# Reordering the first ramp of a three-layer transformer kernel: four buffers for rounded weights, parts of gate/up behind their own weight groups

## The reference, cut to what matters

```python
def fp4_quant_dequant(x):                       # blocks of 16 along the last dimension
    scale = max(max(abs(block)) / 6, 1e-12)
    q = GRID[searchsorted(MID, abs(block / scale))] * sign(block) * scale
    # GRID 0 .5 1 1.5 2 3 4 6
def fp4_linear(x, w):
    return einsum('bsk,nk->bsn', fp4_quant_dequant(x), fp4_quant_dequant(w))
def ffn(x):
    h = silu(fp4_linear(x, w_gate)) * fp4_linear(x, w_up)     # 256 -> 704
    return fp4_linear(h, w_down)                              # 704 -> 256
x = x + 0.5 * ffn(layernorm(x))
x = x + attention(layernorm(x))                 # complex projections Wq, Wk, Wv, Wo with biases
x = x + 0.5 * ffn(layernorm(x))
```

## Time and profile before

| | |
|---|---|
| Median of 3 runs | 894.83 us (894.54 to 894.95) |
| The profiled execution | 895.14 us, span 893.3 us |
| TensorE busy | 872.8 us, 98% of the span |
| VectorE busy | 708.2 us, 79% |
| ScalarE busy | 626.4 us, 70% |
| POOL busy | 570.5 us, 64% |
| Chain that ended last | TensorE 93% of the span |

### The profile page before, as it was taken

One profiled execution on the slowest core, in us unless ns is written; L12 is line 12 of the kernel. 1 busy time (PEld: TensorE's weight loads), 2 busy tenths in 40 slices (PEclk: granted clock), 3 DMA queues, 4 the chain that ended last, 5 costly groups with the idle time before them and its releaser, 6 DMA issues.

```text
span 893.3 us, 14660 instructions
## 1 busy us (share of the span) xinstructions
PE 872.8 (98%) x4836; PEld 753.7 (84%) x4836; DVE 708.2 (79%) x1104; ACT 626.4 (70%) x1394; POOL 570.5 (64%) x640
## 2 busy tenths in 40 slices
PE   4999999999999999999999999999999999999997
PEld 3788999999988788888888788888888999999996
DVE  6987999999977897855656646455688999999997
ACT  5889888987685866758686786758775676555543
POOL 5477889988640554536658454636676878877762
PEclk9999999999999999999999999999999999999999
DMA  9200000000000000000000000000000000000001
GB/s 313 73 1 1 1 1 1 2 1 1 1 1 1 1 1 1 0 1 1 1 1 1 1 1 1 1 1 1 1 1 1 1 25 25 24 25 25 1 24 48
DMA packets 11948, 13.73 MB, mean 15 GB/s; under 512 B 864, under 2 KB 11104, under 8 KB 11872
## 3 DMA queue, kind: packets, MB, share of 16 engines
q1 hardware_dynamic: 11872, 12.79, 4.3%
HBM read 8.59 MB, written 4.19 MB: 14 GB/s over the span
## 4 chain that ended last, share of the span: by engine, by line
PE 93%; DVE 2%; ACT 2%; DMA 1%; issue 1%; POOL 0%; SPq 0%; DVEq 0%; ACTq 0%; POOLq 0%
PE bank L2035 27%; PE bank L2299 20%; PE bank L2362 19%; PE bank_b L2046 7%; PE bank L1912 7%; PE bank_b L2053 5%; PE bank L2289 2%; PE bank L2107 1%; PE bank_b L2107 1%; DMA wk_s<-in_L_attn_Wk 1%; PE bank L1908 1%; PE bank L1919 1%; PE bank_b L1912 0%; ACT s_ring L1738 0%; DVE grid L915 0%
## 5 line engine op out<-in xcount | busy, mean ns | idle before, releaser
L690 POOL TENSOR_TENSOR p_lo<-s_ring,p_hi 128x512 fp32r<-128x512 f32 x128 | 167.1, 1309 | 186.3 <-ACT p_hi L1749 185.8
L638 POOL TENSOR_TENSOR zq<-grid,s_neg 128x256 f32<-128x256 f32 (+2 forms) x184 | 142.2, 802 | 12.8 <-DVE grid L915 12.0
L2035 PE MATMUL bank<-w_hi,T_hi 128*128 128x512 f32 (+1 forms) x384 | 149.7, 390 | 0.2 <-DVE z L874 0.2
L2035 PE MATMUL bank<-w_lo,T_hi 128*128 128x512 f32 (+1 forms) x384 | 144.0, 375 | 0.0
L2035 PE MATMUL bank<-w_hi,T_lo 128*128 128x512 f32 (+1 forms) x384 | 144.0, 375 | 0.0
L2362 PE MATMUL bank<-p_hi,xv 128*128 128x512 f32 x512 | 141.1, 393 | 0.3 <-DVE p_lo L1074 0.3
L1092 DVE TENSOR_TENSOR top<-bank,top 128x512 f32<-128x512 f32 x92 | 63.4, 690 | 93.5 <-ACT s_ring L1732 91.8
L1732 ACT ACTIVATE s_ring<-bank 128x512 f32<-128x512 f32 x128 | 76.0, 594 | 73.4 <-PE bank L2299 66.9
L1537 ACT ACTIVATE T_hi<-bank 128x1024 fp32r<-128x1024 f32 (+1 forms) x68 | 64.7, 952 | 80.6 <-PE bank L1912 80.3
L2362 PEld LDWEIGHTS bank<-p_hi,xv 128*128 128x128 f32 x512 | 94.0, 188 | 18.6 <-issue 0.7
L620 POOL TENSOR_TENSOR y<-z,s_inv 128x960 f32<-128x960 f32 (+1 forms) x56 | 99.8, 1782 | 6.6 <-DVE rounded L909 5.9
(11 more groups left out here) (242 smaller groups left out, 1926.9 us busy)
## 6 DMA issues: line engine op xcount, KB each, us to landing
out<-x SPq DMA_DIRECT2D x7, 512.0 KB, 2.9
x<-in_L_attn_hidden_states SPq DMA_DIRECT2D x3, 1024.0 KB, 12.2
x<-in_L_attn_hidden_states SPq DMA_DIRECT2D x2, 512.0 KB, 7.5
wraw<-in_L_ffn_w_down SPq DMA_DIRECT2D x1, 704.0 KB, 7.5
wraw<-in_L_ffn_w_up SPq DMA_DIRECT2D x1, 640.0 KB, 5.5
wq_s<-in_L_attn_Wq SPq DMA_DIRECT2D x1, 512.0 KB, 7.1
wk_s<-in_L_attn_Wk SPq DMA_DIRECT2D x1, 512.0 KB, 8.0
wo_s<-in_L_attn_Wo SPq DMA_DIRECT2D x1, 512.0 KB, 8.4
```

Of the source, the lines that this page charges most:

```text
L638: last = nc.gpsimd.tensor_tensor(out=blocks(zq[:, to:to + hi - lo]), in0=blocks(grid[:, lo:hi]), in1=spread(s_neg[:, par, lo // BLOCK:hi / ...
L690: nc.gpsimd.tensor_tensor(out=lower_buf(n, c), in0=score_buf(n, c), in1=upper_buf(n, c).bitcast(F32), op=ALU.subtract).then_inc(plo_done, 1)
L2035: last = nc.tensor.matmul(gu[:, lo:hi], lhsT=T[:, par, HK + kd, :], rhs=w[:, kd, lo:hi], start=n == 0, stop=n == len(terms) - 1)
```

## The change

- wy gets four buffers. All six weight_y run on POOL (0 to 3 first, ahead of weight_q(0); 4 and 5 behind first_ffn(-4)), none on VectorE; weight_y(i) waits for the rounding of piece i - 4, and one semaphore counts them.
- The addition of eps leaves POOL for the first two groups: ScalarE does it for tiles 0 to 3, VectorE for tiles 4 to 7, between first_blocks(-3) and weight_grid(5).
- VectorE: weight_scales is split in weight_maxima and weight_inverses; for the down weights the rounding of chain step -3 stands between the two.
- ScalarE: weight_abs(2) between the variances of tiles 1 and 2; all four sums of tiles 4 to 7 ahead of upper_group(0); normalise(0) ahead of upper_group(1); chain_upper(-4) and chain_rest(-4) ahead of upper_group(5) and lower_group(4); lower_group(5) behind m_upper, m_lower behind it and normalise(2) behind that.
- TensorE: transpose_group(0) and (1) ahead of key_query_rest(0); chain_lower(-4) ahead of weight_lower(5); gate_up(0, 0) waits for 4 lowered groups, gate_up(0, 1) for 5, gate_up(0, 2) for all; query_row(2) and (3) behind gate_up(0, 1).

The diff, cut to its core:

```diff
-        wy = sb("wy", [P, 2, I], at=ffn)
+        wy = sb("wy", [P, 4, I], at=ffn)
...
             def group_std(g):
-                if g != 2:
+                if g > 2:
                     pool.wait_ge(x_var, input_variances(4 * g + 3))
                     nc.gpsimd.tensor_tensor(out=var[:, q], in0=var[:, q], in1=eps_all[:, q],
                                             op=ALU.add).then_inc(x_eps, 1)
+                if g != 2:
                     pool.wait_ge(x_eps, g + 1 if g < 2 else g)
...
             def weight_y(i):
                 pool.wait_ge(wc["inv"], SCALED[i])
-                if i >= 2:
-                    pool.wait_ge(wc["abs"], i - 1)
-                    pool.wait_ge(wc["rnd"], i - 1)
+                if i >= 4:
+                    pool.wait_ge(wc["abs"], i - 3)
+                    pool.wait_ge(wc["rnd"], i - 3)
...
-            weight_y(0)
-            weight_y(1)
-            weight_y(2)
+            for i in range(4):
+                weight_y(i)
             weight_q(0)
             weight_q(1)
             group_std(0)
...
             first_ffn(-4, 0)
-            pool.wait_ge(wc["y"], 2)
+            weight_y(4)
             weight_y(5)
             group_std(1)
...
+            def variances_with_eps(g):
+                q = slice(4 * g, 4 * g + 4)
+                dve.wait_ge(x_var, 4 * g + 4)
+                nc.vector.tensor_scalar(out=var[:, q], in0=var[:, q], scalar1=EPS, scalar2=None,
+                                        op0=ALU.add).then_inc(x_eps, 1)
...
             weight_grid(0)
             weight_grid(1)
-            weight_y(3)
             weight_grid(2)
             weight_grid(3)
             first_blocks(-6, 0)
             first_blocks(-5, 1)
             dve.wait_ge(wd_in, 16)
-            weight_scales(4, 4, NW)
-            first_blocks(-4, 0)
-            weight_y(4)
+            weight_maxima(4, NW)
+            first_to_grid(-3)
+            weight_inverses(4, 4, NW)
+            first_scales(-2, 0)
+            first_scaled(-2)
             first_product(0)
             weight_grid(4)
             first_blocks(-3, 1)
+            variances_with_eps(1)
             weight_grid(5)
...
+            def first_variances_with_eps():
+                act.wait_ge(x_var, 4)
+                nc.scalar.activation(var[:, 0:4], var[:, 0:4], ACT.Copy, bias=EPS).then_inc(x_eps, 1)
...
-            x_variances(0, 4)
+            x_variances(0, 2)
             weight_abs(2)
+            x_variances(2, 4)
+            first_variances_with_eps()
             weight_abs(3)
-            x_sums(4, 6)
+            x_sums(4, 8)
             upper_group(0)
+            normalise(0)
             upper_group(1)
-            normalise(0)
             lower_group(0)
             lower_group(1)
-            x_sums(6, 7)
             upper_group(2)
             upper_group(3)
...
+            chain_upper(-4, 0)
             upper_group(5)
-            chain_upper(-4, 0)
+            chain_rest(-4, 0)
             lower_group(4)
-            lower_group(5)
-            chain_rest(-4, 0)
             absolute(-3)
             m_upper()
+            lower_group(5)
+            m_lower()
             normalise(2)
-            x_sums(7, 8)
-            m_lower()
             minus_means(1)
             silu_gate(0)
...
             key_query_product()
-            key_query_rest(0)
             transpose_group(0)
             transpose_group(1)
+            key_query_rest(0)
             key_query_rest(1)
...
             query_row(1)
+            chain_lower(0, -4, 0)
             weight_lower(5)
-            chain_lower(0, -4, 0)
-            query_row(2)
-            query_row(3)
-            pe.wait_ge(wc["lo"], G1)
+            pe.wait_ge(wc["lo"], 4)
             wait_lowered(0, -4)
             gate_up(0, 0)
             key_query_lower()
+            pe.wait_ge(wc["lo"], 5)
             gate_up(0, 1)
+            query_row(2)
+            query_row(3)
             transpose_chain(0, -3)
+            pe.wait_ge(wc["lo"], G1)
             pe.wait_ge(aw["m_lo"], 1)
             gate_up(0, 2)
```

More of the change, by code:

```diff
@@ L197, in macaron_kernel @@
         x_in_s = [sem(f"x_in{n}") for n in range(len(x_parts))]
-        wc = {k: sem("w_" + k) for k in ("amax", "up", "neg", "inv", "y", "y_pool", "abs", "rnd", "grid", "q", "T", "hi",
+        wc = {k: sem("w_" + k) for k in ("amax", "up", "neg", "inv", "y", "abs", "rnd", "grid", "q", "T", "hi",
                                          "sub", "lo")}
@@ L422, in weight_groups @@
                        wd_hl[:, k:k + 2, 0:D], wd_hl[:, k:k + 2, D:], NW)
-        Y_MADE = {0: ("y_pool", 1), 1: ("y_pool", 2), 2: ("y_pool", 3), 3: ("y", 1), 4: ("y", 2), 5: ("y_pool", 4)}
         SCALED = (1, 2, 3, 3, 4, 4)
@@ L557, in weight_y @@
                 pool.wait_ge(wc["inv"], SCALED[i])
-                if i >= 2:
-                    pool.wait_ge(wc["abs"], i - 1)
-                    pool.wait_ge(wc["rnd"], i - 1)
-                nc.gpsimd.tensor_tensor(out=blocks(wy[:, i % 2, :]), in0=blocks(wraw[:, i * I:(i + 1) * I]),
+                if i >= 4:
+                    pool.wait_ge(wc["abs"], i - 3)
+                    pool.wait_ge(wc["rnd"], i - 3)
+                nc.gpsimd.tensor_tensor(out=blocks(wy[:, i % 4, :]), in0=blocks(wraw[:, i * I:(i + 1) * I]),
                                         in1=spread(wsm[:, 3, i * HB:(i + 1) * HB], HB),
-                                        op=ALU.mult).then_inc(wc["y_pool"], 1)
+                                        op=ALU.mult).then_inc(wc["y"], 1)
             def bias_column():
@@ L811, in _, with weight_maxima @@
             dve.wait_ge(sixths, 2)
-            def weight_scales(n, first, last):
+            def weight_maxima(first, last):
                 c = slice(first * HB, last * HB)
@@ L816, in weight_scales, with weight_inverses @@
                                         op=ALU.max, apply_absolute_value=True).then_inc(wc["amax"], 1)
+            def weight_inverses(n, first, last):
+                c = slice(first * HB, last * HB)
                 dve.wait_ge(wc["amax"], n)
@@ L824, in weight_scales @@
                 dve.wait_ge(wc["inv"], n)
-            def weight_y(i):
-                if i >= 2:
-                    dve.wait_ge(wc["abs"], i - 1)
-                    dve.wait_ge(wc["rnd"], i - 1)
-                nc.vector.tensor_tensor(out=blocks(wy[:, i % 2, :]), in0=blocks(wraw[:, i * I:(i + 1) * I]),
-                                        in1=spread(wsm[:, 3, i * HB:(i + 1) * HB], HB),
-                                        op=ALU.mult).then_inc(wc["y"], 1)
+            def variances_with_eps(g):
[3 more added lines that the diff above has]
+                                        op0=ALU.add).then_inc(x_eps, 1)
             def weight_grid(i):
                 wabs_i = wabs[i % 2 if i < 4 else 0]
-                made, count = Y_MADE[i]
-                dve.wait_ge(wc[made], count)
+                dve.wait_ge(wc["y"], i + 1)
                 dve.wait_ge(wc["abs"], i + 1)
@@ L840, in weight_grid @@
                     dve.wait_ge(wc["grid"], i)
-                nc.vector.scalar_tensor_tensor(out=wrnd[:], in0=wabs_i, scalar=ROUND, in1=wy[:, i % 2, :],
+                nc.vector.scalar_tensor_tensor(out=wrnd[:], in0=wabs_i, scalar=ROUND, in1=wy[:, i % 4, :],
                                                op0=ALU.max, op1=ALU.add).then_inc(wc["rnd"], 1)
@@ L1019, in ffn_step @@
                 return step, blocks_of, product, residual_last, scales, to_grid, scaled, lower
-            first_ffn, first_blocks, first_product, first_residual_last, *_ = ffn_step(0)
+            (first_ffn, first_blocks, first_product, first_residual_last, first_scales, first_to_grid, first_scaled,
+             _) = ffn_step(0)
             second_ffn, _, second_product, _, scales, to_grid, scaled, second_lower = ffn_step(1)
             dve.wait_ge(gate_in, 16)
-            weight_scales(1, 0, 1)
+            weight_maxima(0, 1)
+            weight_inverses(1, 0, 1)
             dve.wait_ge(mixed_in, 16 * 3)
-            weight_scales(2, 1, 2)
+            weight_maxima(1, 2)
+            weight_inverses(2, 1, 2)
             dve.wait_ge(up_in, 16)
-            weight_scales(3, 2, 4)
+            weight_maxima(2, 4)
+            weight_inverses(3, 2, 4)
             weight_grid(0)
             weight_grid(1)
-            weight_y(3)
             weight_grid(2)
@@ L1329, in weight_abs @@
             def weight_abs(i):
-                made, count = Y_MADE[i]
-                act.wait_ge(wc[made], count)
+                act.wait_ge(wc["y"], i + 1)
                 if i >= 2:
                     act.wait_ge(wc["grid"], i - 1 if i < 5 else i)
-                nc.scalar.activation(wabs[i % 2 if i < 4 else 0], wy[:, i % 2, :], ACT.Abs,
+                nc.scalar.activation(wabs[i % 2 if i < 4 else 0], wy[:, i % 4, :], ACT.Abs,
                                      scale=ROUND).then_inc(wc["abs"], 1)
```

## The result

The changed kernel takes 895.89 us as a median of 20 runs (895.26 to 897.40), the kernel before 894.81 us in the 20 runs beside them (894.37 to 895.38). The ratio is 1.0014, with an interval of 1.0008 to 1.0021: 1.1 us slower, which is clear of the interval but inside the 0.2% that the text ahead took as no change. The prediction was 895.6 us.

What follows compares the result with a forecast made beforehand. The ramp bounds the kernel: TensorE's matmuls until 31.7 us, then VectorE's list until 49.1 us. Profiled 895.14 + 0.8 (of it 0.2 from product(0)) - 0.31 = 895.6 us as a median; range 894.0 to 897.0 us.

Steps and rivals of the forecast that it cites:

- TensorE's stretch: TensorE's matmuls from 12.8 to 31.7 us, up to product(0): product(0) 0.1 to 0.3 us later, taken as 0.2.
- the list of signs: Times and waits expected in the new trace, such as gate_up(0, 0) at 26.1 and product(0) at 31.8 to 32.0 us.
- the power: POOL's power for tiles 4 to 7, behind VectorE's eps addition: not before 36.5 us, taking 1.20 us (1.04 to 1.20).
- that sign: At VectorE's product(0): a start ahead of 31.4 us would show the prediction wrong.
- TensorE's wait ahead of the transposes: Ahead of the first transposes, TensorE waits for weight_q(1) from 16.38 to about 16.85 us, 0.47 us.
- The term that was off is the first: On TensorE ahead of product(0): gate_up(0, 0) starts at about 26.15 in place of 27.05 us, 0.9 us earlier.
- VectorE's stretch: VectorE's list from 31.7 to 49.1 us: the eps addition delays the maxima, 0.9 us later, 0.2 of it from product(0).
- The 0.31: In the final sum: the median, 894.83 us, lies 0.31 us below the profiled execution, 895.14, so 0.31 is subtracted.
- (1): Ahead of product(0): TensorE's waits do go, product(0) up to 1.3 us earlier, 894.2 us; chance 0.18.
- (2): TensorE's early matmuls: a 0.47 us wait makes the clock rise later, 1.7 us over the forecast, 897.3 us; chance 0.12.
- (3): Ahead of product(0): POOL's weight_y(4) and (5) hold VectorE's scaled(-2), product(0) 0.2 to 0.4 us later still, 896.0 us; chance 0.14.
- (4): Whole ramp: nothing lasts, the eps addition costs only 0.1 us and TensorE's wins and losses cancel, 894.9 us; chance 0.14.

Runs made afterwards that it cites:

- the control: The kernel before, unchanged, profiled a second time; its clock rose 3.9 us after TensorE's first matmul, tile 1's gate/up at 19.33 us after that matmul.
- after: The changed kernel with the whole change, against the kernel before: median 895.89 us, ratio 1.0014.
- The first trace: The kernel before, unchanged, in the profile that the prediction used: 895.14 us, clock rising 6.2 us after TensorE's first matmul.
- e10: The changed kernel with one wait added: POOL starts weight_y(5) only behind VectorE's scaled(-2); 895.30 us (1.0014).
- e2: The changed kernel with key_query_rest(0) put back ahead of transpose_group(0) and (1); 895.82 us (1.0014).
- e9: The changed kernel with POOL adding eps for tiles 4-7, query_row(2), (3) behind value_output_product(1), weight_y(5) behind scaled(-2), weight_q(5) behind tile 1's inverses; 894.32 us (0.9998).
- e11: The changed kernel itself run and traced once more, nothing altered; 895.53 us (1.0014).

## Why the prediction was right

**The frame held.** The end moves as the ramp moves: +0.86 at tile 2, +0.86 at the last matmul. The ramp has TensorE's stretch up to product(0) and VectorE's list behind it. The absolute times in the list of signs did not hold: gate_up(0, 0) came at 25.45 us for 26.1, the power at 35.89 for 36.5 or later, tile 2's gate/up at 42.52 for 43.4. product(0), at 31.22 us, even lies ahead of the 31.4 that was to show the prediction wrong. All these stood on a trace with a late start and a late clock. Counted from the first matmul that sign was at 31.4 - 12.83 = 18.57 us, and product(0) came at 18.67; the control, with the clock of after, has it at 18.29. The waits named among the signs are there: VectorE's idle time ahead of the maxima (0.32 us for about 0.5), and TensorE's wait ahead of the transposes.

**TensorE's stretch.** The forecast was a product(0) 0.1 to 0.3 us later, taken as 0.2; by the control it is 0.37 later, with the sign and the reason right (gate_up(0, 0) starts earlier, the rows cost it again). The term that was off is the first: gate_up(0, 0) came 0.70 us earlier, not 0.9. The first trace, counted in the same way, would say 1.32, but it had the late clock. And the stretch from it to product(0) grew by 0.37 + 0.70 = 1.07 us, 0.96 for the rows and 0.1 for the change of form, of which the forecast had up to 0.2. weight_q(1) ended at 16.35 us for 16.61, by its own path as worked out, since the loads of this execution landed 0.25 us earlier. The wait ahead of the transposes was 16.40 - (12.55 + 3.55) = 0.30 us, not 0.47, as the hand-over from POOL took 0.05 us and not 0.24.

**VectorE's stretch.** The forecast was 0.7 us from the addition (0.9 less product(0)'s 0.2, with bounds of 0.45 and 0.8); it is 0.47. The chain ran as described: VectorE's place, POOL's power, nmr, normalise(4), maxima. The addition started 35.65 - 31.22 = 4.43 us behind product(0), where the text had 36.37 - 31.93 = 4.44. From there to the maxima it put 2.43 us, and 37.85 - 35.65 = 2.20 it was. The mis-sized term is the power, 1.01 us, near the short one of the two durations in the earlier trace rows, for which I had taken the long one, 1.20. The traces show that this is no chance: it took 1.01 us in all seven traces that have the addition on VectorE, where it starts behind VectorE's scaled(-1), and 1.12 to 1.20 us in the seven others, where scaled(-1) comes in the middle of it. By moving the addition the change also moved the power. This error and product(0)'s, of opposite signs, nearly cancel, which is luck: 0.8 us forecast, 0.86 in the traces.

**The number.** 895.14 + 0.8 - 0.31 = 895.6 for a measured 895.89. The 0.31 took the profiled execution for slightly slow; it was (a late clock, 0.6 us), and quick between 480 and 490 us (0.5 us). What the sum lacked is the fall of the clock. The 13 runs of after in which it stays have a median of 895.74, and all 20 have 895.89.

**The rivals.** (1) The waits of TensorE did not go: product(0) is later. (2) The clock did not rise late; the pair of key_query_rest at 19.33 us runs at full pace, 0.44 us to the next start. It falls, though, in some executions, at 42.7 to 44.0 us, and not because of the wait that I named: e2, without that wait, has it too. The page of the Trainium skill cited for this rival, "TensorE: Matmul & The Clock Gate", says under "What's actually happening" that the clock follows recent activity; these traces agree in that each fall stands behind TensorE's thin stretch, though in after's the same stretch left the clock up. I had looked for breaks only ahead of the rise. (3) The port did hold scaled(-2), 1.30 us for 0.42, and it was covered, as e10 shows. (4) was wrong: the addition cost 0.5 us, not 0.1.

## What to carry to other kernels

When a small operation moves to an engine with a full list, price its place in that list and follow its consumers back to the same engine: here one addition of 0.07 us cost 0.5 us in both directions, and left a break in TensorE's work behind which the clock fell in some executions. Small matmuls that fill a wait are worth keeping in it: where they left it, the wait behind them came bare, and in their new place they held up TensorE and ScalarE. And read shifts of under a microsecond only against two traces of the old kernel, counted from the first event that the kernel does not control.

## What the runs showed of the hardware that I had not expected

- **One collision between VectorE and POOL holds a short instruction until the long one ends.** VectorE instructions with two inputs in SBUF went from 0.22 to 1.41, 0.42 to 1.30 and 0.20 to 0.70 us when a POOL instruction had started just ahead of them; with POOL's kept back until behind it (e9) s_up took 0.22 us. The Trainium skill says so in "SBUF — State Buffer", "Who interferes with whom": the one that issues first keeps the shared ports for its whole instruction. These three cases agree; the addition at 480 us, 0.69 or 1.44 us, has a POOL instruction under way at its start in both traces, and what tells them apart was not found. What surprised me is the leverage. A gain of 0.7 us elsewhere moved two starts past each other by 0.05 us and 1.2 us was lost there.
- **The granted clock can fall in the middle of a busy kernel.** In e11 it stood at the lower level for 3.4 us after TensorE had been thinly busy from 41.0 to 42.7 us (0.68 of 1.70 us), and cost 1.6 us. In after it stayed behind the same stretch (0.64 of 1.70 us). Of the 168 runs of kernels with a shorter break none shows a fall.
- **Two executions of one kernel differ by 0.6 us in the ramp** by the time at which the clock rises (3.9 or 6.2 us after the first matmul), and by 0.5 us between 480 and 490 us, 0.3 of it at the addition beside POOL's instructions. What decides either was not tried.
